# A windowed-attention and convolution block: new order of work on every engine, single wide matmul tiles for four stages, one transfer moved to another queue

## The reference

```python
def _attention(xw, ...):                      # xw: windows x 49 tokens x 96 channels
    xn = _layernorm(xw, ln_g, ln_b)
    qkv = (xn @ qkv_w.T + qkv_b).reshape(Bw, N, 3, HEADS, HEAD_DIM)   # 12 heads of 8
    attn = jnp.einsum('bhnd,bhmd->bhnm', q * SCALE, k) + bias
    attn = jax.nn.softmax(attn, axis=-1)
    out = jnp.einsum('bhnm,bhmd->bhnd', attn, v)
    return out @ proj_w.T + proj_b
...
seq = x + attention(x)
conv = depthwise 3 x 3 convolution of seq, padding 1
bn = (conv - bn_mean) * bn_g * rsqrt(bn_var + EPS) + bn_b
h = gelu(bn @ w1.T + b1)                      # 96 -> 384
out = bn + (h @ w2.T + b2)                    # 384 -> 96
```

## Time and profile before

| what | value |
|---|---|
| median of 3 runs | 3448.92 us (3444.31 to 3459.77) |
| the profiled execution | 3444.23 us |
| its span in the trace | 3442.4 us |
| granted TensorE clock, mean | 0.992 |
| TensorE matmul busy | 3098.5 us, 90% |
| VectorE busy | 3071.3 us, 89% |
| ScalarE busy | 2833.2 us, 82% |
| GpSimd busy | 1999.8 us, 58% |

### The profile page before, as it was taken

How to read it: one execution, slowest core, us unless ns; L and a number is a source line. 1 busy time by engine, 2 the same in 40 slices (tenths; PEclk the granted TensorE clock), 3 DMA queues, 4 the chain that set the end, 5 groups by cost and what they waited for, 6 DMA issues and landing times.

```text
span 3442.4 us, 213611 instructions
## 1 busy us (share of the span) xinstructions
PE 3098.5 (90%) x94988; PEld 2172.5 (63%) x94988; DVE 3071.3 (89%) x4907; ACT 2833.2 (82%) x4883; POOL 1999.8 (58%) x2574
## 2 busy tenths in 40 slices
PE   3899989989989889899899898999998998998996
PEld 2666666666666666666666666666666666666663
DVE  4889989989989889899899898999998998999995
ACT  3888888878888888888888888888888888888885
POOL 2565656656656556566565565565655665656654
PEclk9999999999999999999999999999999999999998
DMA  1232322323323223233232233232322332322321
GB/s 38 81 91 80 91 87 84 91 81 89 90 80 92 86 84 89 81 88 88 82 89 85 86 88 88 86 89 86 91 82 86 87 88 84 88 86 87 90 84 35
DMA packets 269976, 289.20 MB, mean 84 GB/s; under 512 B 55651, under 2 KB 252580, under 8 KB 269062
## 3 DMA queue, kind: packets, MB, share of 16 engines
q1 hardware_dynamic: 236294, 198.40, 20.7%
q0 software_dynamic: 32768, 77.14, 6.5%
HBM read 39.34 MB, written 38.54 MB: 23 GB/s over the span
## 4 chain that ended last, share of the span: by engine, by line
PE 75%; DVE 11%; issue 8%; POOL 4%; ACT 1%; SPq 0%; POOLq 0%; DMA 0%; ACTq 0%; DVEq 0%
PE d_ps L256 22%; PE b_ps L256 16%; PE a_ps L256 12%; PE sm_ps L315 8%; PE st_ps L294 8%; PE o_ps L340 8%; DVE s L739 5%; POOL sl L631 2%; DVE mx L713 2%; DVE y L776 1%; POOL sh L624 1%; DVE kl L747 1%; DVE ql L747 1%; DVE ximg L795 1%; POOL ox L615 0%
## 5 line engine op out<-in xcount | busy, mean ns | idle before, releaser
L739 DVE SCALAR_TENSOR_TENSOR s<-ximg,cols,s 96x392 f32<-96x392 f32 x1792 | 1351.3, 754 | 44.1 <-POOL s L604 7.8
L713 DVE TENSOR_REDUCE mx<-sm_ps 128x12 f16<-128x588 f32 x1024 | 778.8, 761 | 57.1 <-PE sm_ps L315 53.0
L600 POOL TENSOR_TENSOR s<-ximg,cols 96x392 f32<-96x392 f32 x256 | 216.3, 845 | 969.9 <-DVE y L776 969.7
L468 ACT ACTIVATE p<-st_ps 128x588 f32<-128x588 f32 x1024 | 672.0, 656 | 82.7 <-PE st_ps L294 45.5
L315 PEld LDWEIGHTS sm_ps<-k_all,q_all 127*49 127x49 f16 x24576 | 493.5, 104 | 306.3 <-issue 228.9
L256 PE MATMUL d_ps<-g,w_s 128*64 128x392 f32 x3072 | 671.2, 506 | 3.6 <-ACT g L519 2.7
L615 POOL DMA_DIRECT2D ox<-o_sb x1024 | 582.6, 572 | 36.2 <-ACT o_sb L493 16.5
L294 PE MATMUL st_ps<-q_all,k_all 128*49 128x49 f16 x24576 | 541.1, 185 | 61.9 <-issue 56.9
L294 PEld LDWEIGHTS st_ps<-q_all,k_all 128*49 128x49 f16 x24576 | 479.4, 103 | 181.0 <-issue 97.6
L315 PE MATMUL sm_ps<-k_all,q_all 127*49 127x49 f16 x24576 | 526.6, 186 | 53.4 <-issue 48.9
L340 PE MATMUL o_ps<-p,v 128*32 128x49 f32 x24576 | 400.6, 210 | 33.5 <-issue 31.7
(11 more groups left out here) (114 smaller groups left out, 6122.4 us busy)
## 6 DMA issues: line engine op xcount, KB each, us to landing
ox<-o_sb POOLq DMA_DIRECT2D x1024, 73.5 KB, 2.3
k_all<-kh SPq DMA_DIRECT2D x512, 75.0 KB
q_all<-qh SPq DMA_DIRECT2D x512, 75.0 KB
x_sb<-in_x SPq DMA_DIRECT2D x256, 147.0 KB, 2.7
out<-y SPq DMA_DIRECT2D x256, 147.0 KB
k_all<-kl SPq DMA_DIRECT2D x256, 75.0 KB
q_all<-ql SPq DMA_DIRECT2D x256, 75.0 KB
q_all<-mxt SPq DMA_DIRECT2D x256, 9.4 KB, 2.0
```

Of the source, the lines that this page charges most:

```text
L468: af(p32[:, p, :, :].rearrange("p (b h) n -> p b h n", b=2), st_ps[:, :, 0:HALF].rearrange("p b (h n) -> p b h n", n=TOK), ACT.Exp).then_i ...
L713: v.tensor_reduce(mx[:, c % 2, :, p].rearrange("p (b h) -> p b h", b=2), sm_ps[:, :, 0:HALF].rearrange("p b (h n) -> p b h n", n=TOK), AX. ...
L739: v.scalar_tensor_tensor(acc, image_rows(c, k // 3, k % 3), cw_c[:, k:k + 1], acc, ALU.mult, ALU.add)\
```

## The change

The loops of all engines are ordered anew, with other leads for some stages. `centred`, `variance`, `values` and `projection` use one matmul with 96 or 128 columns of weights in place of two halves. `values` now writes b_ps; `variance` and `hidden` 2 write a_ps. The second pair of values times p is split: part 2 runs in the chunk's own step behind `second` 1, part 3 in the next. `to_channels` goes from GpSimd to SP's queue. `image_high` stands one step later on GpSimd. On ScalarE the table load, exp 3 and the high parts of keys and queries head the step; on VectorE the last maximum `maxima(s - 1, 0)` ends it.

```diff
-STEPS = CHUNKS + 8
+STEPS = CHUNKS + 10
@@ SP
+            def to_channels(c):
+                wait(sp, proj_done, c - 2)
+                wait(sp, o_done[0], c)
+                wait(sp, o_done[1], c)
+                for x4 in range(4):
+                    sp.dma_start(ox[:, c % 2, x4, :], o_sb[x4::4, c % 2, :, :]).then_inc(o_in[c % 2], 16)
             for s in range(STEPS):
+                term(k_all, 0, kh, kh_done, s - 2)
+                load(s)
+                store(s - 10)
+                term(q_all, 0, qh, qh_done, s - 2)
+                term(k_all, 1, kl, kl_done, s - 2)
                 term(q_all, 2, ql, ql_done, s - 2)
-                term(q_all, 0, qh, qh_done, s - 2)
-                load(s)
+                to_channels(s - 5)
                 maximum_row(s - 3)
-                first_term(k_all, 0, kh, kh_done, s - 1)
-                term(k_all, 2, kh, kh_done, s - 1)
+                first_term(k_all, 2, kh, kh_done, s - 1)
                 term(q_all, 1, qh, qh_done, s - 1)
-                term(k_all, 1, kl, kl_done, s - 1)
-                store(s - 8)
@@ TensorE
+            def whole_three(o, sh, sl, mh, ml):
+
+                mm(o, sh, mh, start=True, stop=False)
+                mm(o, sh, ml, start=False, stop=False)
+                return mm(o, sl, mh, start=False, stop=True)
...
-                halves(d_ps[0:128, 0:CT], center[:, :], x_sb[:, at:at + CT]).then_inc(xc_done, 1)
+                mm(d_ps[0:C, 0:CT], center[:, 0:C], x_sb[:, at:at + CT], start=True, stop=True).then_inc(xc_done, 1)
...
-                halves(b_ps[0:128, 0:CT], avg[:, :], sq[:, :]).then_inc(var_done, 1)
+                mm(a_ps[0:C, 0:CT], avg[:, 0:C], sq[:, :], start=True, stop=True).then_inc(var_done, 1)
...
-                    last = halves_three(a_ps[:, 0:NP * C].rearrange("p (h n d) -> p n h d", n=NP, d=HD)[:, n], s_h, s_l,
+                    last = whole_three(b_ps[:, 0:NP * C].rearrange("p (h n d) -> p n h d", n=NP, d=HD)[:, n], s_h, s_l,
                                       wq_h[0:C, 2 * C:], wq_l[0:C, 2 * C:])
...
-                    last = halves(o, wp[:, :], ox[:, c % 2, w, :].rearrange("c (n r k) -> c n r k", n=NP, k=WS))
+                    last = mm(o, wp[:, 0:C], ox[:, c % 2, w, :].rearrange("c (n r k) -> c n r k", n=NP, k=WS), start=True, stop=True)
...
-            hidden_ps = {0: b_ps, 1: d_ps, 2: b_ps}
+            hidden_ps = {0: b_ps, 1: d_ps, 2: a_ps}
...
             for s in range(STEPS):
-                values_times_p(s - 4, 2)
+                exp_scores(s - 3, 0)
+                values_times_p(s - 4, 3)
                 centred(s)
+                exp_scores(s - 3, 1)
                 max_scores(s - 2, 2)
-                exp_scores(s - 3, 1)
                 values(s - 2)
                 variance(s)
                 exp_scores(s - 3, 2)
                 values_times_p(s - 3, 0)
+                max_scores(s - 2, 3)
+                projection(s - 5)
+                hidden(s - 7, 0)
                 values_times_p(s - 3, 1)
-                max_scores(s - 2, 3)
-                hidden(s - 7, 0)
-                projection(s - 5)
                 hidden(s - 7, 1)
                 maxima_rows(s - 2)
                 exp_scores(s - 3, 3)
                 hidden(s - 7, 2)
                 second(s - 7, 1)
+                values_times_p(s - 3, 2)
                 keys(s)
+                queries(s)
+                max_scores(s - 1, 0)
                 second(s - 7, 2)
-                max_scores(s - 1, 0)
                 second(s - 7, 0)
-                queries(s)
                 max_scores(s - 1, 1)
-                exp_scores(s - 2, 0)
-                values_times_p(s - 3, 3)
@@ ScalarE
             for s in range(STEPS):
+                act.preload_act_table_set("natural_log_exp_and_others")
+                exp(s - 4, 3)
+                key_high(s - 1)
+                query_high(s - 1)
+                log_sums(s - 5)
                 exp(s - 3, 0)
-                log_sums(s - 5)
+                outputs(s - 4, 1)
+                square(s)
                 inverses(s - 5)
-                square(s)
-                outputs(s - 4, 1)
                 exp(s - 3, 1)
                 log_variance(s)
+                root(s)
                 exp(s - 3, 2)
-                root(s)
                 act.preload_act_table_set("gelu_and_others")
                 gelu(s - 7, 0)
                 input_high(s)
                 gelu(s - 7, 1)
+                outputs(s - 3, 0)
                 gelu(s - 7, 2)
-                outputs(s - 3, 0)
-                act.preload_act_table_set("natural_log_exp_and_others")
-                exp(s - 3, 3)
-                key_high(s)
-                query_high(s)
@@ GpSimd
             for s in range(STEPS):
+                image_high(s - 7)
                 image_low(s - 7)
-                to_channels(s - 4)
                 input_low(s)
                 first_tap(s - 5)
-                image_high(s - 6)
@@ VectorE
             for s in range(STEPS):
-                maxima(s - 2, 0)
+                key_low(s - 1)
                 block_out(s - 8)
-                key_low(s - 1)
                 maxima(s - 2, 1)
+                tap(s - 7, 7)
                 query_low(s - 1)
-                tap(s - 7, 7)
                 tap(s - 7, 8)
+                normalise(s - 5)
                 maxima(s - 2, 2)
+                values_out(s - 2)
                 tap(s - 6, 2)
-                values_out(s - 2)
-                normalise(s - 5)
                 input_normal(s)
                 maxima(s - 2, 3)
+                tap(s - 6, 3)
+                image_sum(s - 5)
                 maxima_out(s - 2)
-                image_sum(s - 5)
-                tap(s - 6, 3)
                 tap(s - 6, 4)
                 tap(s - 6, 5)
                 tap(s - 6, 6)
+                maxima(s - 1, 0)
```

More of the change, by code:

```diff
@@ L227, in maximum_row @@
                              mxt[:, c % 2, :, :].rearrange("m w t -> m (w t)")).then_inc(row_in[c % 2], 16)
+            def to_channels(c):
+                if not real(c):
+                    return
+                wait(sp, proj_done, c - 2)
[3 more added lines that the diff above has]
+                    sp.dma_start(ox[:, c % 2, x4, :], o_sb[x4::4, c % 2, :, :]).then_inc(o_in[c % 2], 16)
             def store(c):
@@ L356, in variance @@
                 wait(pe, sq_done, c)
[L357 to L358 removed]
+                free(pe, (ql_done, c-1), (g_done[2], c-8), (sum_done, c-6), (lnv_done, c-1))
+                mm(a_ps[0:C, 0:CT], avg[:, 0:C], sq[:, :], start=True, stop=True).then_inc(var_done, 1)
             def queries(c):
@@ L363, in queries @@
                 wait(pe, xl_done, c)
-                free(pe, (sum_done, c-5), (v32_done, c-2), (ql_done, c-1))
+                free(pe, (g_done[2], c-7), (sum_done, c-5), (lnv_done, c+0), (ql_done, c-1))
                 halves_three(a_ps[0:128, 0:CT], wq_h[:, 0:128], wq_l[:, 0:128], xh[:, c % 2, :, 0:TOK], xl[:, c % 2, :, 0:TOK]).then_inc(q_done, 1)
@@ L370, in keys @@
                 wait(pe, xl_done, c)
-                free(pe, (g_done[2], c-7), (g_done[0], c-7), (lnv_done, c+0), (kl_done, c-1))
+                free(pe, (g_done[0], c-7), (v32_done, c-2), (kl_done, c-1))
                 halves_three(b_ps[0:128, 0:CT], wq_h[:, 96:224], wq_l[:, 96:224], xh[:, c % 2, :, 0:TOK], xl[:, c % 2, :, 0:TOK]).then_inc(k_done, 1)
@@ L405, in hidden @@
                 if k == 0:
-                    free(pe, (lnv_done, c+7), (kl_done, c+6), (g_done[2], c-1), (g_done[0], c-1))
+                    free(pe, (v32_done, c+5), (kl_done, c+6), (g_done[0], c-1))
                 elif k == 1:
@@ L409, in hidden @@
                 elif k == 2:
-                    free(pe, (g_done[0], c+0), (lnv_done, c+7), (kl_done, c+6), (g_done[2], c-1))
+                    free(pe, (sum_done, c+2), (lnv_done, c+7), (ql_done, c+6), (g_done[2], c-1))
                 halves_three(hidden_ps[k][:, 0:CT], w1_h[:, k * 128:(k + 1) * 128], w1_l[:, k * 128:(k + 1) * 128], sh[:, :], sl[:, :]).then_inc(hid_done[k], 1)
@@ L489, in outputs @@
                     return
-                wait(act, pv_done[1 if half == 0 else 2], c)
+                wait(act, pv_done[1 if half == 0 else 3], c)
                 if half == 0:
@@ L518, in gelu @@
                 wait(act, s_done[k], c - 1)
-                af(g[:, k, :], {0: b_ps, 1: d_ps, 2: b_ps}[k][:, 0:CT], ACT.Gelu, bias=b1_c[:, k:k + 1], scale=1 / UP).then_inc(g_done[k], 1)
+                af(g[:, k, :], {0: b_ps, 1: d_ps, 2: a_ps}[k][:, 0:CT], ACT.Gelu, bias=b1_c[:, k:k + 1], scale=1 / UP).then_inc(g_done[k], 1)
             def square(c):
@@ L533, in log_variance @@
                 wait(act, var_done, c)
-                af(rstd[:, :], b_ps[0:C, 0:CT], ACT.Ln, bias=eps_c).then_inc(lnv_done, 1)
+                af(rstd[:, :], a_ps[0:C, 0:CT], ACT.Ln, bias=eps_c).then_inc(lnv_done, 1)
             def root(c):
@@ L604, in first_tap @@
```

(13 more changed lines are left out.)

8 lines of the change are left out of this document (4 added, 4 removed).

## The result

The changed kernel takes 3558.09 us (median of 4 runs, 3555.84 to 3562.15); the kernel before took 3446.78 beside it (4 runs, 3444.31 to 3459.77). The ratio is 1.0326, with an interval of 1.0305 to 1.0348: 3.3% slower. Forecast were 3375 us, in a range of 3270 to 3510 that does not hold it.

The account below looks back on a forecast made before the run. TensorE's stages and stalls, with ScalarE's chain as second limit, were taken to bound the kernel. 5.4 + 7.0 = 12.4 us, plus 0.35 of stalls, gives 12.75 per step from 13.03: 70 us less, 3375 us, range 3270 to 3510.

Parts of the forecast that it names:

- Banks: Hidden 2 and variance go to a_ps, values to b_ps: nothing on the path freed, no price, but no slack.
- I let it pay those 0.6: VectorE: the normalisation follows into GpSimd's addition, where tap 8 fell before, and pays 0.6 us.
- VectorE's work stays at 11.87, under 12.4: hidden: VectorE's 11.87 us of work per step fits in the 12.4 us step, with 0.5 us of slack.
- Halts: TensorE stalls for unfetched instructions: with matmuls less dense, most vanish, 0.35 of 1.05 us per step staying.
- widths cost and the stalls stay: Rival, slower: width changes cost and all TensorE stalls remain, 3554 us; with half of the excess 3500; chance 0.22.
- Widths: TensorE: 13 tile-width changes per step instead of 4, some 0.1 us each, 0.9 us more; work from 11.2 to 12.2.
- ScalarE's chain: 5.4 us from variance to second(1), then 7.0 us of uncovered TensorE work to the next variance: 12.4 us.
- the rival of free widths: Rival: 128-wide tiles on TensorE change for free, 160 us less, 3285 us; chance 0.2.
- Whole tiles: Centre, values, variance, projection on TensorE: equal array time, 20 fewer matmuls and loads, longer loads costing 0.1 us per step.
- Take-over by VectorE: Rival, no change: y and hidden 0 lost their slack, TensorE waits at the centre; 3430 to 3460 us; chance 0.13.
- the signs named for "right": Trace: width gaps of 0.1 us, issue under 5%, values 0.5 to 0.65, no mxt wait, normalisation 1.1, second(1) awaiting gelu 1.
- the signs for "wrong": Trace: issue 8% or more, TensorE waiting for y at centre or sl at hidden 0, mxt behind to_channels on SP's queue.

Follow-up runs that it names:

- the bank: Changed kernel with hidden 2 and its gelu back in bank b_ps: 3474.8 us, ratio 1.0106.
- the normalisation: Changed kernel with the normalisation behind maximum 2 on VectorE instead of ahead of it: 3488.2 us, ratio 1.0110.
- both together: Changed kernel with hidden 2 back in b_ps and the normalisation behind maximum 2: 3377.5 us, ratio 0.9790.
- bank, normalisation, halves and pair: Changed kernel with hidden 2 in b_ps, normalisation later, all four stages as halves, part 2 in a pair ahead of part 3: 3447.7 us, ratio 1.0019.
- the same, part 2 in the pair: Changed kernel with hidden 2 in b_ps, normalisation later, and part 2 of values times p in a pair ahead of part 3: 3399.8 us, ratio 0.9874.
- the same, halves: Changed kernel with hidden 2 in b_ps, normalisation later, and all four stages as halves again: 3376.2 us, ratio 0.9791.
- the same, tap 7 behind query_low: Changed kernel with hidden 2 in b_ps, normalisation later, halves, part 2 in the pair, and tap 7 behind query_low on VectorE: 3464.4 us, ratio 1.0065.

## Why the prediction was wrong

**The step that failed is "Banks": "Nothing on the path is freed ... no price, but no slack".** The text asked what a bank change frees, and what keys, queries and hidden 0 now wait for. It did not ask what hidden 2 itself waits for, which was moved into the bank that the projection fills ahead of it, while the image sum that empties it stands behind twelve VectorE operations, of which y is the first. Stage by stage each wait looked met. Followed round from y to y, the work in series was 13.41 us, more than the 12.75 forecast. Moving only the bank back, or only the image sum forward, recovers 83 or 84 us of the 111.

**The normalisation was sized nearly right and booked wrongly.** "I let it pay those 0.6": it paid 0.8 (1.37 instead of 0.55). But "VectorE's work stays at 11.87, under 12.4: hidden" compares an engine's total with the step. Busy time is 12.1 us per step (901.3 us in 74.5 steps) and does fit; the order did not. The collision stands in both loops, and neither edit alone shows its full worth: the bank gives 83 us, the normalisation 70, both together 181.

**Halts: right in kind, and the gain larger than I took.** I left 0.35 of 1.05 us per step. The halts ahead of matmuls fell from 220.7 us to 2.4. The first rival, "widths cost and the stalls stay", gave 3554 us, 4 from the measured time, and is nevertheless refuted: no stalls stayed, and the halves do not help. A number that fits is no proof of a mechanism. That fewer instructions are worth nothing, by the Trainium skill ("Runtime: NRT & Kernel Launch", Instruction fetch mechanics: crossing a block is mostly hidden), no run here bears out: with the old order kept, whole tiles, with 5% fewer instructions, removed three quarters of the halts and 1.1% of the time.

That the halts are waits for instructions can be read from the traces, by counting in them. With those of its sequencer TensorE has 193048 instructions before and 182808 after, 754.1 and 714.1 times 256; the instruction queue moved 754 and 714 packets. Counted in the order of the trace, the time from one instruction's start to the next gathers at one place of each 256: 418 ns on average before, 24 after, which is no more than at the other places, 132 in the kernel before with whole tiles, and 332 with bank, normalisation, halves and pair. Where this time is over 0.2 us (374 of the 754 blocks before), the instruction behind it starts 1.41 us after the latest packet of the instruction queue has landed (1.26 to 1.57 in eight of ten), and 1.40 to 1.45 in the seven other kernels with 80 or more such blocks. A halt ends a fixed time after a packet.

**Widths: right, a little low.** Timeline of the changed kernel, scores with 64 columns and then the first matmul of values with 128:

```profile
1709.95 0.48 PE L332 MATMUL sm_ps<-k_all,q_all 127*49 127x49 f16 x24
1710.36 0.22 PE L278 MATMUL b_ps<-wq_h,xh 96*128 96x96 f16 x1
```

1710.36 - (1709.95 + 0.48 - 0.19) = 0.12 us, where the same width gives 0.03. So 128 against 64 does cost, and the rival of free widths (3285) is out. The centre takes 0.83 us to the next start where halves took 0.71, the variance 0.79 against 0.67, the projection 0.83 against 0.66. The term "TensorE's work goes from 11.2 to 12.2" measured about 12.49 with both loops open (12.69 less the 0.20 of waiting for gelu 1). The 13 changes at 0.12 instead of 0.10 are 0.3 of the difference, and so nearly all of it.

**ScalarE's chain: right, but not the bound of this kernel.** The forecast added 5.4 + 7.0 = 12.4, from the variance to second 1 and back. With both loops open the same path measured 5.39 + 0.14 + 7.16 = 12.69, and it is the bound there. In the changed kernel second 1 starts 0.54 us after gelu 1 and not 0.14: the path has slack, because the loop through the image sum is longer.

**Whole tiles: equal array time, right; longer loads, wrong.** Values take 0.52 us from first start to the variance's, 0.51 before. My 0.1 for longer loads was nothing, see below.

**Take-over by VectorE: the right engine in the wrong place.** That rival looked at the centre and at hidden 0, was priced at 3430 to 3460, and got 0.13. Neither place waits in the trace once the pipeline is filled. A rule of "work per engine" could not have found hidden 2.

**The rest.** The wait ahead of mxt is gone (168.5 us, 2.6 after). to_channels is worth nothing, to within 0.4%. sh no longer waits for tap 8 (167.5 us, 11.6 after), and this is worth nothing either while other loops are longer. The ends cost 7 us more, not 2: 5 of them in filling, which I had not counted. Of the signs named for "right", the widths, the 0.52 us of the values and the lost wait ahead of mxt came; issue is 7% of the chain, not under 5%, but nearly all of it lies between VectorE's operations; and second 1 does not wait for gelu 1. Of the signs for "wrong" none came. No sign named hidden 2.

**What a right prediction would have been.** The step is the longest of: TensorE's work 12.49, ScalarE's chain 12.69, the loop through the image sum 13.41 and the loop through maximum 2 13.05. 13.41 sets it. Most of its terms could be read from the trace of before; the largest that could not is the 1.37, and at the 1.15 forecast the loop would still have been 13.2.

## What to carry to other kernels

When an order or a bank changes, write down for each moved stage everything that its `free` list now waits for, and follow the longest of these round until it comes back to where it began. The work in series on such a loop, across engines, is a lower bound of the step, whatever the engines' busy shares say. Expect a second loop just behind the first: fix and measure them together, since one alone showed 83 or 70 us here and both 181. An engine that counts as busy throughout can still wait: compare the start of a stage with the end of what it needs. And where TensorE issues many short matmuls, how densely they follow each other has a price of its own.

## What the hardware showed that I had not expected

**A whole f16 load is no longer than a narrow one.** The loads of values in the changed kernel, 1000 to 2000 us:

```profile
L278 PEld LDWEIGHTS b_ps<-wq_h,xh 96*128 96x128 f16 x296 | 28.8, 97 | 2.6
```

128 columns take 97 ns, where 64 took 109 and 49 took 103. I had extended the slope of these two to 135. The Trainium skill ("TensorEngine Tiling (Array Packing)", Restrictions) says that column tiling turns off the fast weight load, which would give this picture; no run here tests it.

**VectorE and GpSimd take turns.** A tap went from 0.61 to 0.80 us beside a product and to 1.00 beside sl; GpSimd's product from 0.84 to 1.16, and its cast sh from 0.51 to 0.84. Only the later of two is slowed: sl is 0.93 us with a tap behind it and without. And the later one ends a fixed time after the earlier. A tap or a normalisation that comes behind a GpSimd operation ends 0.42 us after it, in the kernel before as in the changed one, whether it took 0.69, 0.80, 1.00, 1.27 or 1.37 us; the cast ends 0.37 after the normalisation. In the rows above: 1710.73 + 1.15 + 0.42 = 1712.30, and the normalisation ends at 1710.94 + 1.37 = 1712.31. So the later one does little but stand until the earlier is done, and its duration shows only how early it came. Maxima, which read PSUM, took 759 to 762 ns on average in every version. The Trainium skill ("SBUF — State Buffer", Who interferes with whom) has the same division: an operation of VectorE with two inputs in SBUF contends with GpSimd's reads, one with a single SBUF input does not; and it calls the shared ports an exclusive lock. The trace agrees with both.

**Halts depend steeply on density.** Parts 2 and 3 as a pair or apart, and whole tiles or halves, moved the sum of the halts between 3 and 159 us:

| kernel | halts ahead of matmuls, us | step from y to y, median and mean, us |
|---|---|---|
| before | 220.7 | 12.75, 12.96 |
| before, whole tiles | 55.8 | 12.56, 12.81 |
| changed | 2.4 | 13.41, 13.39 |
| changed, part 2 in the pair | 28.2 | 12.99, 13.00 |
| changed, halves | 39.4 | 13.42, 13.40 |
| bank + normalisation | 3.0 | 12.69, 12.68 |
| the same, part 2 in the pair | 43.7 | 12.52, 12.73 |
| the same, halves | 62.9 | 12.50, 12.67 |
| the same, halves and pair | 158.9 | 12.90, 12.92 |
| the same, tap 7 behind query_low | 140.4 | 12.83, 13.00 |

What density is still free stays open: no run varied the number of instructions alone, in steps.
